# One sublayer pair on one core: value weights re-ordered on TensorE, one GpSimd pass gated, layer-norm statistics of one group moved to ScalarE

## The reference, cut to what matters

```python
x = x + tanh(g_xattn) * xattn(layernorm(x), ctx)     # 3 rounds
x = x + tanh(g_ffn)   * ffn(layernorm(x))            # shared FFN + 16 experts, top 512 tokens each

def layernorm(x, eps=1e-5):
    return (x - mean(x)) / sqrt(var(x) + eps)

# xattn: slots = layernorm(x), P = ctx
k, v = rmsnorm(P) @ Wk.T, rmsnorm(P) @ Wv.T
for _ in range(3):
    q = rmsnorm(slots) @ Wq.T
    a = softmax(q k / 16, over the tokens); a = a / (sum over the context + 1e-6)
    slots = gru(a @ v, slots)                        # r, z, n gates; 768 x 256 weights twice
```

## Time and profile before

| | |
|---|---|
| median of three executions | 1107.53 us |
| profiled execution, its own time | 1108.25 us |
| span of the profiled execution | 1106.5 us |
| TensorE busy / VectorE / ScalarE / GpSimd | 1079.6 / 778.8 / 546.2 / 341.7 us |
| mean granted TensorE clock | 0.994 of full speed |

### The profile page before, as it was taken

The page is one execution under the profiler, slowest core; times in us unless marked ns, Lnnn a source line. Parts: engine busy times, 40 slices in busy tenths (PEclk is TensorE's granted clock), DMA queues, the critical chain, the costliest instruction groups (busy, mean ns, idle before and its releaser), DMA issues.

```text
span 1106.5 us, 17708 instructions
## 1 busy us (share of the span) xinstructions
PE 1079.6 (98%) x6087; PEld 930.8 (84%) x6087; DVE 778.8 (70%) x1504; ACT 546.2 (49%) x830; POOL 341.7 (31%) x352
## 2 busy tenths in 40 slices
PE   6899999999999999999999999999999999999996
PEld 4687888888888778888888888988889888888896
DVE  7888687878789877787556666566665666656663
ACT  4455545454447843333555554455454544545442
POOL 6123444444205100000214233343333433324332
PEclk9899999999999999999999999999999999999999
DMA  7601010101226441212663443544434445344421
GB/s 247 153 1 34 6 38 1 39 1 39 79 78 192 149 129 20 38 20 40 194 192 94 134 115 119 148 99 130 132 104 147 107 125 144 92 143 123 111 35 20
DMA packets 61323, 105.39 MB, mean 95 GB/s; under 512 B 12128, under 2 KB 50272, under 8 KB 56928
## 3 DMA queue, kind: packets, MB, share of 16 engines
q1 hardware_dynamic: 43904, 82.78, 23.4%
q0 software_dynamic: 16512, 21.50, 12.0%
q10 hardware_dynamic: 864, 0.55, 0.2%
HBM read 74.11 MB, written 21.27 MB: 86 GB/s over the span
## 4 chain that ended last, share of the span: by engine, by line
PE 92%; DVE 5%; issue 1%; DMA 1%; ACT 1%; POOL 0%; SPq 0%; DVEq 0%
PE wide L1313 30%; PE wide L867 16%; PE down L1327 16%; PE wide L1162 8%; PE down L1174 4%; PE down L935 3%; PE wide L874 3%; PE wide L876 3%; PE wide L1359 2%; PE side L1299 1%; PE side L1146 1%; PE side L305 1%; PE side L959 1%; PE down L1373 1%; DVE stats L1896 1%
## 5 line engine op out<-in xcount | busy, mean ns | idle before, releaser
L2310 DVE SCALAR_TENSOR_TENSOR hid<-wide,b_up,silu 128x512 f32<-128x512 f32 x120 | 90.1, 751 | 161.4 <-PE wide L1313 154.9
L1313 PE MATMUL wide<-xt_hi,w_hi 128*128 128x512 f32 x480 | 188.4, 392 | 0.0
L1313 PE MATMUL wide<-xt_lo,w_hi 128*128 128x512 f32 x480 | 187.8, 391 | 0.0
L1313 PE MATMUL wide<-xt_hi,w_lo 128*128 128x512 f32 x480 | 186.9, 389 | 0.0
L838 POOL DMA_INDIRECT out_tokens<-y,idx_out x64 | 111.4, 1741 | 220.1 <-DVE y L2291 175.0
L1690 ACT ACTIVATE silu<-wide,b_gate 128x512 f32<-128x512 f32 x120 | 82.1, 684 | 143.7 <-PE wide L1313 143.7
L1327 PE MATMUL down<-w_hi,hid_hi 128*128 128x256 f32 x480 | 136.5, 284 | 0.0
L1327 PE MATMUL down<-w_lo,hid_hi 128*128 128x256 f32 x480 | 135.7, 283 | 0.0
L1327 PE MATMUL down<-w_hi,hid_lo 128*128 128x256 f32 x480 | 135.7, 283 | 0.0
L1699 ACT ACTIVATE hid_hi<-hid 128x512 fp32r<-128x512 f32 x120 | 76.0, 633 | 100.2 <-DVE hid L2310 100.2
L2261 DVE TENSOR_TENSOR w_lo<-raw,w_hi 128x768 fp32r<-128x768 f32 x128 | 121.4, 949 | 2.5 <-ACT w_hi L1664 2.5
(11 more groups left out here) (329 smaller groups left out, 2266.9 us busy)
## 6 DMA issues: line engine op xcount, KB each, us to landing
raw<-in_w_expert SPq DMA_DIRECT2D x32, 1536.0 KB, 6.8
x_raw<-in_x SPq DMA_DIRECT2D x16, 256.0 KB, 6.8
out_tokens<-slots SPq DMA_DIRECT2D x16, 256.0 KB, 3.8
token_rows<-work SPq DMA_DIRECT2D x8, 512.0 KB, 3.0
out_tokens<-y POOLq DMA_DIRECT2D x8, 512.0 KB, 6.0
attn<-rms_c SPq DMA_DIRECT2D x24, 128.0 KB, 2.3
attn<-expo SPq DMA_DIRECT2D x22, 128.0 KB, 2.3
x_first<-in_x SPq DMA_DIRECT2D x8, 256.0 KB, 3.2
```

The costliest lines, as they stand in the source:

```text
L1313: last = nc.tensor.matmul(bank[:, f % 2, :], w[f // HALF_F][:, f % HALF_F, (c + k) * P:(c + k + 1) * P], x_[:, k, :], start=(m == 1), stop ...
L2310: nc.vector.scalar_tensor_tensor(hid[:, f % 2, :], eup[:, f % 2, :], b_up[:, bass.ds(e, 1), f:f + 1].rearrange("p a b -> p (a b)"), silu[: ...
```

## The change

Four edits. First, the mean and variance of the four blocks of group 1 leave VectorE (four `bn_stats`, four aggregates) and are made by ScalarE in two passes over each block: an Identity pass with scale 1/256 whose accumulator is the mean, a small copy that scales the four means by -1/16, and a Square pass with scale 1/16 and that bias, whose accumulator is the variance. They stand on ScalarE behind `pn_t` and ahead of `kp_t`. VectorE waits for the eleventh increment of `c_act` instead of the second.

Second, the order of the value weights changes on TensorE and ScalarE, and with it their PSUM banks. Number 1 moves behind the first spread of the RMS factors, number 2 behind the first part of the first GRU unit, number 3 behind the column sums; the second spread moves between the two halves of the scores. ScalarE's copies follow the same order, and its exponential now stands ahead of the copies of numbers 2 and 3 and of `own_weights(1)`.

Third, GpSimd's pass over group 2 in round 1 also waits for `v_recd` 2, which is VectorE's second reciprocal in two parts (L1774).

Fourth, in the last round `subtract_hi(0)` goes ahead of `turn_slots(4)`, and `turn_slots(5)` ahead of `turn_h(2)`.

```diff
+        neg_mean = gates("neg_mean", [P, BLK])
+        unused = Region(O + 189440, O + 197632)("unused", [P, 2 * BLK, D])
...
-            small_banks = (side[:, 1, :], down[:, 0, :], down[:, 1, :], side[:, 0, :])
-            vw_bank = (1, 2, 3, 0)
+            small_banks = (side[:, 1, :], down[:, 0, :], down[:, 1, :], side[:, 0, :], gate_x)
+            vw_bank = (1, 3, 3, 4)
...
                         pool.wait_ge(s_ss, run - 1)
+                        if run == G + 2:
+                            pool.wait_ge(v_recd, 2)
                         multiply(g)
...
                 value_weights(0)
-                value_weights(1)
                 pe.wait_ge(e_w, 3)
                 turn_rms(0)
                 turn_first(1)
                 turn_first(3)
                 spread_rms(0, 0)
-                value_weights(2)
-                spread_rms(0, 1)
+                value_weights(1)
                 pe.wait_ge(a_whi, B)
                 pe.wait_ge(p_wlo, B)
-                pe.wait_ge(e_w, 5)
+                pe.wait_ge(e_w, 4)
                 scores(0, 0, (2, 4), True, (0,))
+                spread_rms(0, 1)
                 scores(0, 0, (2, 4), True, (1,))
-                pe.wait_ge(a_rms, 2)
-                value_weights(3)
                 pe.sem_inc(s_ss, G)
                 pe.wait_ge(p_wlo, B + 2)
                 gru_unit(0, 0, 0, 0, None, ("first",))
-                pe.wait_ge(e_w, 7)
+                pe.wait_ge(e_w, 5)
+                value_weights(2)
                 column_sums(0)
+                value_weights(3)
                 turn_rec(0)
...
                 def turn_and_subtract():
+                    subtract_hi(0)
                     turn_slots(4, (v_x1, 2))
-                    subtract_hi(0)
...
+                turn_slots(5, (v_x1, 5))
                 turn_h(2, (a_hlo, 2))
-                turn_slots(5, (v_x1, 5))
...
+                BY_SCALAR = range(BLK, 2 * BLK)
+                act.wait_ge(l_x[1], 32)
+                for t in BY_SCALAR:
+                    nc.scalar.activation(unused[:, t - BLK, :], x_blk(1, t - BLK), ACT.Identity, scale=1.0 / D,
+                                         accum_out=mv0[:, t, 0:1]).then_inc(c_act, 1)
+                act.wait_ge(c_act, 2 + BLK)
+                nc.scalar.activation(neg_mean[:, :], mv0[:, BLK:2 * BLK, 0], ACT.Copy, scale=-float(D) ** -0.5)\
+                    .then_inc(c_act, 1)
+                act.wait_ge(c_act, 2 + BLK + 1)
+                for t in BY_SCALAR:
+                    nc.scalar.activation(unused[:, t, :], x_blk(1, t - BLK), ACT.Square, scale=float(D) ** -0.5,
+                                         bias=neg_mean[:, t - BLK:t - BLK + 1], accum_out=mv0[:, t, 1:2]).then_inc(c_act, 1)
...
                 value_weights(0)
-                value_weights(1)
-                copy_rms(0, 0, True)
                 first_high(1)
                 first_high(3)
+                copy_rms(0, 0, True)
                 copy_rms(0, 1, True)
+                value_weights(1)
                 own_weights(0)
+                exponentials(0)
                 value_weights(2)
                 value_weights(3)
-                exponentials(0)
                 own_weights(1)
...
-                for g in range(G1):
+                for g in (0, 2, 3):
                     first_stats(range(g * BLK, (g + 1) * BLK))
                     aggregate(range(g * BLK, (g + 1) * BLK))
-                dve.wait_ge(c_act, 2)
+                dve.wait_ge(c_act, 2 + 2 * BLK + 1)
```

## The result

The change makes the kernel slower: 1114.03 us median of four runs (1112.36 to 1114.78) against 1107.70 us (1107.29 to 1108.12) for the kernel before on the same chip, ratio 1.0056 with the 95% interval 1.0042 to 1.0070, so 6.3 us. The forecast was 1108.3 us, and its range ended at 1110.2.

A forecast was written before the change was run, and what follows sets the result against it. TensorE was taken to bound the kernel (92% of the chain). Start +0.2, hold -0.6 and turns +1.2 made +0.8 us on the profiled 1108.25, or 1108.3 against the median; range 1105.2 to 1110.2.

The forecast's parts named there:

- Start: Up to 64.3 us: first attention -0.2, clock +0.85, hole -0.43, in all +0.2 us, ends -1.6 and +1.1.
- Scores and all behind them come 1.2 us earlier: Start: with value weights 1 moved, groups 1 and 3 are turned when VectorE's low parts are ready; 1.2 us earlier.
- With TensorE fed I take it at full: Start: `turn_rec` and `spread_rec`, at half clock before, run at full clock; 0.2 and 0.75 us less.
- The step from `own_weights(1)` on: Before the first attention: `own_weights(1)` 3.4 us later, its four DMAs ahead of the attention's; gain there only 0.2 us.
- now waits up to its end: Before the first attention: VectorE's small operation waits for GpSimd's subtraction until 43.8; low part 0.65 us earlier, not 1.6.
- Clock at the restart: First attention: TensorE idles 4.2 us, half clock may follow; 0.85 us lost, between nothing and 1.65.
- Hold: Ahead of 101.46 us: holding GpSimd's pass frees VectorE's copy; gain 0.6 us, bounds 0 and 0.85.
- Statistics: Start: group 1's statistics on ScalarE make VectorE's chain 0.41 us earlier, not 1.70, at no cost.
- Turns: Last round: the new order makes TensorE go on at 367.3 instead of 366.07; loss 1.2 us, bounds 0.3 and 2.9.
- rival B: Half clock right at the first attention's restart and again after the hole before `turn_slots(5)`: +3.25, 1110.8 us; chance 0.13.
- The base: Profiled execution of the kernel before, 1108.25 us, taken as starting point, 0.72 above the median of 1107.53.

The follow-up runs named there:

- e3: The kernel before with only the new order of the value weights (second edit); 1111.72 us, ratio 1.0043.
- e2: The changed kernel without its turn order (fourth edit); ratio 1.0029 against the kernel before, its trace not read.
- e1: The kernel before with only the turn order (fourth edit, both turns swapped); 1110.54 us, ratio 1.0031.
- e6: The kernel before with only `turn_slots(5)` moved ahead of `turn_h(2)`; 1110.36 us, ratio 1.0019.
- e12: The whole change with SyncE's spreads and `own_weights(1)` behind the first attention, and twenty extra transposes ahead of `turn_slots(5)`; 1109.98 us, ratio 1.0019.
- e5: The change without its turn order, with SyncE's four spreads of pair 1's own value weights issued behind the first attention DMAs; 1110.26 us, ratio 1.0019.
- e9: As e5, with ScalarE's `own_weights(1)` also moved behind its attention DMAs; 1109.25 us, ratio 1.0013.
- e11: The kernel before with only GpSimd's one pass held (third edit); 1107.00 us, ratio 0.9994.
- e4: The kernel before with only the statistics by ScalarE and the held GpSimd pass (first and third edits); 1107.12 us, ratio 0.9997.
- e8: As e1, with twenty overwritten extra transposes put into TensorE's hole ahead of `turn_slots(5)`; 1108.74 us, ratio 1.0002.
- e7: The kernel before with only `subtract_hi(0)` moved ahead of `turn_slots(4)`; 1108.32 us, ratio 0.9999.

## Why the prediction was wrong

**Start, forecast +0.2 us; in the two traces +2.30 at the first attention and -0.43 at 64.3, so +1.9.** By the times it cost more: e3, its order alone, +4.3, and e2 +3.2 with the hold's -0.5 in it, so about 3.7. Of the 5.5 us between forecast and result some 3.5 are here and 2 in the turns. Three steps failed.

"Scores and all behind them come 1.2 us earlier": in the changed kernel's trace the sums start 0.55 later than before. I had moved the transposes up without their input: TensorE waits for VectorE's low part (2.35 us idle ahead of 24.29), and the low clock, which in before fell on value weights that nobody waited for, fell on these transposes (3.07 us instead of 1.91). In e3 the clock stayed full there, and still nothing was won. With the old order the transposes wait for the same low part, as e1 shows:

```profile
24.27 2.19 PE L1024 MATMUL wide<-ident,x_raw 128*128 128x128 f32 x16 [0.68 <-DVE slots_lo L1945]
```

In e3 that wait is 2.18 us. Counted from the first statistics of VectorE (6.24 in e3, 6.99 in e1, 6.17 in e6) the sums start after 30.7 us in e3 and after 30.8 in e1 and e6. Value weights 1 had stood in a wait and cost nothing there; taking it out won 0.1 us, not 1.2, and left TensorE idle.

"With TensorE fed I take it at full" was wrong in every trace of the value weights' order (e2's is not read) but e12's: the clock reads 0.50 from 43 to 48 us in the changed kernel, although TensorE was busy from 39 to 42 without a gap. `spread_rec` took its 1.22 us.

The step from `own_weights(1)` on was right in kind and too small. The forecast had its end at 41.9, the DMAs at 41.95 to 44.4 and the attention at 48.1, 6.2 us later; in the trace they are 43.85, 43.88 to 46.28 and 50.66, 6.8 us later. Most of the error is thus the date of the start, not the length behind it. The rule that a ring is consumed in order (the Trainium skill, DMA: Bandwidth & Descriptors, Queues, rings and completion order) agrees with the traces: SyncE's first attention DMA lands 3.7 us after its issue behind the weights', and 2.2 us after it in e5, where none stand ahead. But e5 shows that taking the ring away wins nothing at the first attention as long as ScalarE's half comes later. The block of L2021 is 0.5 us of that. I had it in the text ("now waits up to its end"; the usual 0.17 us stands not in the earlier trace rows, but e9 shows 0.16) and counted it as a smaller gain instead of as part of the limit; the 0.9 us by which ScalarE's DMA lands later I did not have at all.

**Clock at the restart, forecast +0.85.** In the traces it is all or nothing: 3.4 us at 0.50 in e3 (49.9 to 53.3) and e12 (47.5 to 50.9), 1.7 lost each; nothing in the changed kernel's own profile, where the low stretch ended inside the idle time. This may be why the profiled execution is the shortest of its kernel, 1112.36 where the three without a profile took 1113.62 to 1114.78. That those have the low stretch at the restart is argued from e3 and e12 and not seen, since they have no trace.

**Hold, forecast -0.6, measured -0.5** (e11 median, and e4 against e8 in the traces), by the mechanism forecast: the CAST freed, L1749 held instead.

**Statistics, forecast a 0.41 us earlier chain.** VectorE was 0.67 earlier, of which 0.16 is an earlier first load: from its first statistics to `var` it takes 6.84 us before and 6.33 now, so 0.5 by the edit. Nothing of it arrived: e4 with them is no faster than e11 without.

**Turns, forecast +1.2, bounds 0.3 and 2.9; measured +3.2 alone (e1), +2.7 between the traces.** The order was worth 0.95 to 1.4 (e8), near the forecast. The step that failed was the value taken for the clock, nothing, though the text gave its price as 1.65; it measured 1.6. In its own words rival B "decides if both low stretches begin where TensorE starts again". The one of the turns came in e1, e6 and the changed kernel, beginning between 0.6 us ahead of the restart and 1.4 behind it; the one of the first attention came in e3 and e12 and not in the changed kernel's profile. I had given B 0.13, because the trace of before left open where a low stretch falls. The one hole of that size which the trace held, 2.54 us, was followed by half clock, and I gave it no weight in the turns. B's 1110.8 is itself 3.2 us short, since it keeps the start's gain of 0.2.

**The range.** The prediction's own bounds did not reach the result, and the range was narrower than they are. The start's upper end is not +1.1: 0.3 late at the attention, 1.65 and -0.43 make 1.5. With 2.9 for the turns and nothing from the hold that is 1111.9, while the range ended at 1110.2.

**The base.** The profiled execution of before has the first attention at 48.36. The other traces with that order have 46.77 to 47.83 (e1, e4, e6, e7, e8, e11), so against the usual execution the changed kernel's 50.66 is 2.8 to 3.9 us late and not 2.3. That profiled execution carries the idle time and half clock of 16 to 24 us and is 0.7 us above its median, so a part of each "earlier" in my working was already there in the usual execution.

## What to carry to other kernels

An idle stretch of TensorE costs itself and then what half clock does to the work behind it; in this kernel 3.4 us of half clock, worth about 1.6 us, behind holes of 2.3 to 2.8 us. Before moving a wait, add up the waits that it joins: two of 0.6 us with work between them were free of it here, one of 2.8 was not, and useless transposes in the hole were worth 1.6 (traces) to 2 us.
Moving a step later moves all that hangs on it past what stood behind it: one ScalarE line brought four DMAs and a GpSimd pass into the same 2 us as the attention, and only moving the line itself, beyond the attention, gave the stretch back; the pass then held VectorE's next chain by 1.5 us.
Work that stands in another engine's wait is free: before moving it out, look at what ended the idle time behind it.

## What the runs showed of the hardware

Waits of TensorE ahead of the second turn, and the granted clock in the stretch behind it: 2.80 us (the change), 2.73 (e1) and 2.27 (e6) were followed by 0.50; 1.48 and then 0.56 (e5, turns unchanged) by 0.50 as well; 1.03 and 0.56 (e7) and 0.60 and 0.56 (before) by 1.00; 2.35 us of filler and a wait of 0.46 (e8) by 1.00. e5 shows that the half clock can come there without the edit. Each of these low stretches lasted 3.4 us.

In the first 20 us the granted clock column does not tell everything. In the changed kernel the eight matmuls with `wv` took nearly twice as long as in the kernel before (3.78 us against 1.99), and the column reads 1.00 in both. The groups of the changed kernel, 12.0 to 15.8 us, and its stretch:

```profile
L1059 PE MATMUL down<-pn_t,wv_sb 128*128 128x256 f32 x8 | 3.8, 651 | 1.5 <-DMA wv_sb<-in_wv_t 1.5
```

```profile
12.10:15.80 3.70, 3.70 (x9) 2.95 (x10) 3.29 (x20) 0.70 (x3) 0.61 (x3) 1.00 1.03 394
```

and the group of the kernel before, 12.0 to 14.3 us:

```profile
L1055 PE MATMUL down<-pn_t,wv_sb 128*128 128x256 f32 x8 | 2.0, 392 | 1.8 <-DMA wv_sb<-in_wv_t 1.8
```

It is 1.99 us in e1 and e6, 3.44 to 3.78 in e3, e4, e5 and e7 to e11, with the same code or a changed start alike. In e12 it is 2.70, and there the column does read 0.50, from 13.3 to 16.7 us. What slows the others is not shown.
